# An exact LSTM solved by sweeps: the convergence test moved from the end of a sweep to its step 44

## What is computed

```python
x_proj = jnp.einsum('btd,gd->btg', x, W_ih) + b_ih + b_hh
def step(carry, xp):
    h, c = carry
    gates = xp + h @ W_hh.T
    i, f, g, o = jnp.split(gates, 4, axis=-1)
    c = jax.nn.sigmoid(f) * c + jax.nn.sigmoid(i) * jnp.tanh(g)
    h = jax.nn.sigmoid(o) * jnp.tanh(c)
    return ((h, c), h)
_, hs = jax.lax.scan(step, (h0, c0), jnp.swapaxes(x_proj, 0, 1))
```

## Time and profile before

| | |
|---|---|
| median of 3 runs | 2495.29 us (2492.91 to 2497.29) |
| the profiled execution | 2494.4 us |
| its span in the trace | 2492.6 us |
| mean granted TensorE clock | 0.953 of full speed |
| busy: PE, PE weight loads | 88%, 76% |
| busy: DVE, ACT | 69%, 60% |
| matmuls of the sweeps, line 746 | 4800 records, 602.6 us busy |

### The profile page before, as it was taken

The page is one execution under the profiler, slowest core; times in us unless marked ns, Lnnn a source line. Parts: engine busy times, 40 slices in busy tenths (PEclk is TensorE's granted clock), DMA queues, the critical chain, the costliest instruction groups (busy, mean ns, idle before and its releaser), DMA issues.

```text
span 2492.6 us, 43835 instructions
## 1 busy us (share of the span) xinstructions
PE 2193.6 (88%) x13739; PEld 1884.3 (76%) x13739; DVE 1716.5 (69%) x3984; ACT 1504.2 (60%) x3023; POOL 156.2 (6%) x156
## 2 busy tenths in 40 slices
PE   4678989999999999999989899988888888888834
PEld 2457877888888888888878688878887888788723
DVE  5755878777777777777747777765655656555685
ACT  2344448888888878888843366655554555455515
POOL 2333000000000000000000000000000000000060
PEclk7789999999999999999999999999999999999975
DMA  3212320000000000000043122223332333233203
GB/s 93 80 63 82 94 95 20 28 22 28 26 25 25 28 27 25 25 29 24 22 123 93 36 99 112 104 108 113 114 114 84 114 115 107 90 115 115 74 2 101
DMA packets 94279, 174.11 MB, mean 70 GB/s; under 512 B 8088, under 2 KB 68500, under 8 KB 93858
## 3 DMA queue, kind: packets, MB, share of 16 engines
q1 hardware_dynamic: 62914, 86.59, 10.6%
q10 hardware_dynamic: 28108, 81.19, 10.4%
q0 software_dynamic: 3136, 4.76, 0.7%
HBM read 114.14 MB, written 58.36 MB: 69 GB/s over the span
## 4 chain that ended last, share of the span: by engine, by line
PE 52%; DVE 19%; ACT 8%; issue 8%; ACTq 2%; DMA 2%; DVEq 1%; POOL 0%; POOLq 0%
PE psum L600 23%; PE psum L595 11%; PE psum L746 8%; PE psum L703 4%; DVE scr L1542 3%; DVE scr L1540 3%; ACT scr L1012 2%; ACT scr L1020 2%; DMA out_dram<-wq 2%; DVE scr L1538 2%; DVE scr L1336 2%; DVE wp L1432 2%; DVE bufB L1460 1%; DVE bufB L1544 1%; ACTq L1031 1%
## 5 line engine op out<-in xcount | busy, mean ns | idle before, releaser
L920 ACT ACTIVATE counts<-psum 125x500 fp32r<-125x500 f32 (+1 forms) x663 | 719.9, 1121 | 158.3 <-PE psum L595 156.2
L600 PE MATMUL psum<-halves,counts 125*125 125x512 f32 x2500 | 741.9, 417 | 2.5 <-ACT counts L920 2.0
L1362 DVE TENSOR_TENSOR wx<-rs_buf 128x500 bf16<-128x500 bf16 (+2 forms) x1326 | 640.8, 530 | 130.3 <-PE psum L595 76.4
L746 PE MATMUL psum<-bufB,wx 128*128 x4800 | 602.6, 283 | 80.5 <-DVE bufB L1544 71.5
L746 PEld LDWEIGHTS psum<-bufB,wx 128*128 128x128 f32 x4800 | 564.1, 193 | 118.8 <-issue 108.0
L600 PEld LDWEIGHTS psum<-halves,counts 125*125 125x125 f32 x2500 | 416.9, 186 | 59.8 <-issue 4.5
L595 PE MATMUL psum<-wx 128*125 128x250 bf16 x2550 | 398.4, 276 | 5.3 <-DVE wx L1362 5.1
L595 PEld LDWEIGHTS psum<-wx 128*125 128x125 bf16 x2550 | 319.7, 138 | 91.1 <-DVE wx L1362 8.7
L1020 ACT ACTIVATE scr<-scr 128x125 f32<-128x125 f32 x300 | 92.2, 307 | 172.3 <-DVE scr L1542 172.3
L1544 DVE TENSOR_TENSOR bufB<-scr 128x125 f32 (+1 forms) x300 | 87.1, 290 | 146.6 <-ACT scr L1020 146.6
L703 PE MATMUL psum<-bufA,wx 128*128 (+1 forms) x800 | 180.1, 376 | 3.1 <-POOL rs_buf L457 3.1
(11 more groups left out here) (249 smaller groups left out, 2230.4 us busy)
## 6 DMA issues: line engine op xcount, KB each, us to landing
bufA<-gates_of_x ACTq DMA_DIRECT2D x144, 500.0 KB, 3.4
gates_of_x<-bufB SPq DMA_DIRECT2D x24, 1000.0 KB, 3.9
sums_by_feature<-scr SPq DMA_DIRECT2D x51, 125.0 KB, 2.1
x_times_eps_plus_sums<-rs_buf ACTq DMA_DIRECT2D x10, 625.0 KB
wx<-in_x_dram SPq DMA_DIRECT2D x25, 250.0 KB
x_plus_mix<-wx SPq DMA_DIRECT2D x25, 250.0 KB, 4.9
scr<-x_times_eps_plus_sums SPq DMA_DIRECT2D x50, 125.0 KB
x_times_eps_plus_sums<-scr SPq DMA_DIRECT2D x50, 125.0 KB
```

Source lines behind the costliest of these rows:

```text
L600: return mm(psum[0:TP, 3 + v, :], cnt[v][:, hi, :], xhl[:, hi, :, :].rearrange("p s d -> p (s d)"), start=(hi == 0), stop=(hi == NT - 1))
L746: return mm(gate_half(u, m, gate), whhv[:, k, (2 * gate + m) * P:(2 * gate + m + 1) * P], h, start=False, stop=(k == 1), skip_group_check= ...
L920: fn(cnt[v][:, :, 2 * GW * u:2 * GW * u + GW * g].rearrange("p h c -> p c h"), psum[0:TP, u % 3, 0:g * KEYS].rearrange("p (c h) -> p c h", ...
L1362: last = tt(to[:, 0:gs, :, :], tab2[:, 0:k, :].unsqueeze(1).broadcast_to([P, gs, k, 2]), keysT[v][:, part_, g0:g0 + gs, :].unsqueeze(2).br ...
```

## The change

A constant CUT = 44 splits each sweep. `up_to_cut` does steps 0 to 43, `later_step` one of the steps 43 to 49 written out. Before the loop, all three engines do steps 0 to 43 of the first sweep, and DVE copies the states there into a spare buffer (`keep_cut`). One turn of the While loop now does steps 44 to 49 of a sweep, hands the end states on as new starts, does steps 0 to 43 of the next sweep, and then compares the states after step 43 (slot 44 of `hs`, and the cell state) with those that the sweep before had there. Where no element differs by more than the tolerance, the loop ends, and slots 45 to 50 keep what the sweep before wrote. The tolerance is unchanged. The core of the diff:

```diff
+CUT = 44
-        dif = rs_buf[:, 1616 + G4:1616 + G4 + 4 * (CH - 1)].rearrange("p (a j) -> p a j", a=4)
+        dif = rs_buf[:, 1616 + G4:1616 + G4 + 2 * HC].rearrange("p (a j) -> p a j", a=4)
+        at_cut = rs_buf[:, 0:2 * HC].rearrange("p (a j) -> p a j", a=4)
...
+            up_to_cut(0)
             with pe.While(lambda: pe.snap(go) > pe.snap(k_r_)):
-                with pe.Fori(0, LS // 2) as i:
-                    for u in range(2):
-                        time_step(pe.snap(base + 2 * i + u), 2 * i + u, u)
+                for t in range(CUT, LS):
+                    time_step(pe.snap(base + t), t, t % 2)
+                pe.wait_ge(S["st_v"], kv * 3 + 10)
+                up_to_cut(pe.snap(base + LS))
...
+            up_to_cut(0, 0)
             with act.While(lambda: act.snap(go) > act.snap(k_r_)):
+                for t in range(CUT, LS):
+                    later_step(base, before, t)
+                up_to_cut(act.snap(base + LS), act.snap(before + (LS // 2 - 1)))
...
+            def keep_cut():
+                dve.tensor_copy(at_cut[:, 0:2, :], hs[:, CUT, :, :])
+                dve.tensor_copy(at_cut[:, 2:4, :], cN)
+            up_to_cut(0, 0)
+            keep_cut()
...
+                for t in range(CUT, LS):
+                    later_step(base, before, t)
                 dve.wait_ge(S["hh_v"], 2 * base + (2 + 2 * LS))
+                dve.tensor_copy(init_c[:, :, 1:CH], cN[:, :, 0:CH - 1]).then_inc(S["st_v"], 1)
+                dve.tensor_copy(hs[:, 0, :, 1:CH], hs[:, LS, :, 0:CH - 1]).then_inc(S["st_v"], 1)
+                dve.wait_ge(S["st_v"], kv * 3 + 9)
+                dve.tensor_copy(cN, init_c[:, :, :]).then_inc(S["st_v"], 1)
+                dve.wait_ge(S["st_v"], kv * 3 + 10)
+                up_to_cut(dve.snap(base + LS), dve.snap(before + (LS // 2 - 1)))
+                tt(dif[:, 0:2, :], hs[:, CUT, :, :], at_cut[:, 0:2, :], ALU.subtract)
+                tt(dif[:, 2:4, :], cN, at_cut[:, 2:4, :], ALU.subtract).then_inc(S["sw_d"], 1)
...
                 ts(good[:, :], worst[:, :], TOL2, None, ALU.is_le).then_inc(S["sw_v"], 1)
+                keep_cut()
...
+            for v in range(2):
+                dve.wait_ge(S[f"pre_ld{v}"], dve.snap(k_r_) * (8 * LS - 16) + 8 * CUT)
```

More of the change, by code:

```diff
@@ L770, in time_step, with up_to_cut @@
                 half_mm(u, 1, 3, 1, h[1]).then_inc(S["ho_mm"], 1)
+            def up_to_cut(base):
+                for u in range(2):
+                    time_step(base + u if isinstance(base, int) else pe.snap(base + u), u, u)
+                with pe.Fori(1, CUT // 2) as i:
+                    for u in range(2):
+                        time_step(pe.snap(base + 2 * i + u), 2 * i + u, u)
+            up_to_cut(0)
             k_r_, go = pe.alloc_register("pe_sweeps"), pe.alloc_register("pe_go")
@@ L1035, in _, with later_step, up_to_cut @@
             loaded = [[pre_in[v][:, 0:2, :], pre_in[v][:, 2:4, :]] for v in range(2)]
[L1036 to L1043, removed]
+            def later_step(base, before, t):
+                done, u = act.snap(base + t), t % 2
+                if t < LS - 2:
+                    fetch(done, t, u)
+                if t < LS - 1:
+                    act.wait_ge(S[f"pre_ld{1 - u}"], 16 * before + 16 * ((t + 1) // 2))
+                act.wait_ge(S["hth_act"], 2 * done)
+                fill(1 - u, loaded[1 - u] if t < LS - 1 else kept[0])
+                sweep_step(done, u)
+            def up_to_cut(base, before):
                 fetch(base, 0, 0)
+                if not isinstance(base, int):
+                    act.wait_ge(S["hth_act"], 2 * base)
                 fill(1, kept[1])
                 sweep_step(base, 0)
-                with act.Fori(0, LS // 2 - 2) as i:
+                with act.Fori(0, CUT // 2 - 1) as i:
                     for u in (1, 0):
@@ L1055, in _ @@
                         sweep_step(done, u)
[L1056 to L1070, removed]
+                later_step(base, before, CUT - 1)
+            fill(0, kept[0])
+            up_to_cut(0, 0)
+            k_r_, go = act.alloc_register("act_sweeps"), act.alloc_register("act_go")
+            act.reg_mov(k_r_, 0)
+            act.reg_mov(go, CH)
+            with act.While(lambda: act.snap(go) > act.snap(k_r_)):
+                kv = act.snap(k_r_)
+                base = act.snap(kv * LS)
+                before = act.snap(kv * (LS // 2 - 1))
+                for t in range(CUT, LS):
+                    later_step(base, before, t)
+                up_to_cut(act.snap(base + LS), act.snap(before + (LS // 2 - 1)))
                 act.wait_ge(S["flag_v"], kv + 1)
@@ L1553, in _, with later_step, up_to_cut @@
             dve.memset(psum[0:1, 6, 400:401], 0.0).then_inc(S["cnt_z"], 1)
+            cN = tg_c[0][:, 1, :].rearrange("p (c j) -> p c j", c=2)
+            def later_step(base, before, t):
+                u = t % 2
+                if t < LS - 1:
+                    dve.wait_ge(S[f"pre_ld{1 - u}"], 16 * before + 16 * ((t + 1) // 2))
+                fill(1 - u, loaded[1 - u] if t < LS - 1 else kept[0])
+                sweep_step(dve.snap(base + t), t, u)
+            def up_to_cut(base, before):
+                fill(1, kept[1])
+                sweep_step(base, 0, 0)
+                with dve.Fori(0, CUT // 2 - 1) as i:
+                    for u in (1, 0):
+                        t = 2 * i + 2 - u
+                        dve.wait_ge(S[f"pre_ld{1 - u}"], 16 * (before + i) + 16)
+                        fill(1 - u, loaded[1 - u])
+                        sweep_step(dve.snap(base + t), t, u)
+                later_step(base, before, CUT - 1)
+                dve.wait_ge(S["hh_v"], 2 * base + (2 + 2 * CUT))
+            def keep_cut():
[3 more added lines that the diff above has]
+            keep_cut()
             k_r_, go = dve.alloc_register("dve_sweeps"), dve.alloc_register("dve_go")
@@ L1560, in _ @@
                 before = dve.snap(kv * (LS // 2 - 1))
[L1561 to L1570, removed]
```

12 lines of the change are left out of this document (3 added, 9 removed).

## The result

The change takes 2457.77 us, the median of four runs (2454.25 to 2461.89), against 2495.99 us of the kernel before on the same chip (four runs, 2492.91 to 2497.29). The ratio is 0.9845 with a 95% interval of 0.9833 to 0.9858: 38 us less, where 30 were forecast. The profiled execution took 2456.2 us, its span 2454.3.

What follows compares the result with a forecast made beforehand. Bound by a closed PE-ACT-DVE ring, steps times period. Terms 621.3 + 4.8 + 13.4 + 12.2 = 651.7 against 682.75 us; with a shorter passed test and one clock fall 29.9 us less: 2465.0 us, range 2460.0 to 2472.0.

Steps and rivals of the forecast that it cites:

- Three sweeps: Sweeps: the third stays the last and ends at step 43, 144 steps instead of 150; chance 89%.
- the host's 15%: Comparison after step 43 of the third sweep: host calculation gives 1.29e-5 against tolerance 1.526e-5, passing with 15% to spare.
- The closed ring: Each step: PE, ACT and DVE wait in turn, none runs ahead, so a step left out saves its whole period, 4.41 us.
- The handover's working: Step 49 to 0, twice: PE waits for the third copy and starts 2.3 us late; 13.4 us together.
- The failed test: Second sweep, step 43 to 44: the old 12.66 us interval less 0.5 us, so 12.2 us.
- The price of a fourth sweep: Rival, comparison after step 43 of the third sweep fails: one more turn, 233 us, time 2698 us; chance 10%.
- The entry into the While loop: First sweep, step 43 to 44, issued beside DVE's state copies: 0.4 us over a period, 4.8 us.
- item 1: Sweeps' normal periods fall from 147 to 139: 657.43 us becomes 621.3 us.
- One fall out of the two handovers: Handovers, PE idle some 2.6 us: PE's clock falls at one of two, +1.6 us, with 0 and +3.2 as ends.
- The price of 1.6 us: PE's start to first sigmoid after a clock fall: 3.81 us against 2.24, so each fall costs 1.6 us.
- The code fetch at the jump back: While loop's one jump back, behind the failed test: instruction fetch priced between 0 and 3.4 us, taken as 0; chance 15%.
- the Trainium skill's rule on taken branches: While loop's jump back: a taken branch outside a two-page window forces a fetch, so the longer turn would pay there.

Runs made afterwards that it cites:

- The first two experiments: Changed kernel with steps 44 to 47 back in a loop, on PE alone (2458.44 us), then on DVE alone (2463.6 us); one run each.
- the DVE run: Changed kernel with DVE's steps 44 to 47 back in a loop, h written to a slot from a register; 2463.6 us, one run.

## Why the prediction was wrong

**Right.** Three sweeps. The chip's margin after step 43 lies between 0 and 21%, by the run with the tolerance of 1.2e-5; the host's 15% is not measured more closely. The closed ring: each step left out was worth its period, since no other interval grew for it and the run with CUT = 46 was 9.7 us longer for two steps more. The handover's working, 13.4 against 13.24 us, with PE released by the third copy; two small errors in it cancel, a start 0.2 us later than put and steps around it that are shorter. The failed test, 12.2 against 11.68 us: the copies of `keep_cut` did not hold the flag back, and PE starts 1.83 us behind the flag's start (2089.82 - 2087.99) where it took 2127.93 - 2125.69 = 2.24 before. The price of a fourth sweep, 233 us: from first to last sigmoid the run with the tighter tolerance took 886.05 - 647.30 = 239 us more than the change. The entry into the While loop hid under other work nearly altogether, 4.23 us.

**Wrong: item 1, "Normal periods: 147 fall to 139".** I priced all 139 at the old mean of about 4.47 us, though ten of them (44 to 49 in two sweeps) lie between steps that the change writes out. They measured 4.14, and the other 129 the 4.47 put for them. Ten times 0.33 us is 3.3, which is the 3.1 us missing in that term but for 0.2. With them at the old price the median would have been some 2461 us, inside the range. The likely cause can be read from the order of PE's instructions, which I had looked at only for what moved. In the loop the address of h is computed between the wait (line 756 of the changed file) and the matmuls; in a written-out step nothing stands there (this is the order in the program, which no trace records):

```
loop:         L756 ISA / L748 ISA / L748 MATMUL psum<-bufB,wx 128x125 x6
written out:  L756 ISA / L748 MATMUL psum<-bufB,wx 128x125 x6
```

I took the change for a smaller number of the same steps. The first two experiments give the parts, 0.09 us on PE and 0.17 on DVE, and the old kernel with written-out steps had the same 4.14. So it is shown that the looped form of the step costs this, engine by engine. That it is the address and not something else in the looped form is argued from the order and from the later starts; no run keeps the loop and computes the address ahead of the wait.

**Half right: the clock.** "One fall out of the two handovers" is a mean and not what one run does. In the change and the eleven experiments that have handovers there are 26 of them: 13 kept the clock (5.8 to 6.6 us) and 13 lost it (7.0 to 8.3). With an idle time like the change's (2.77 to 2.87 us) it is 7 kept against 12 lost, so that the profiled execution kept both was luck. The price of 1.6 us is near the 1.5 that most falls cost, but two cost 2.7 or 2.8 (8.33 + 5.36 us in the DVE run, 8.33 + 5.44 with the tighter tolerance). What decides is open: an idle time of 2.77 us came out both ways.

**The range.** Its lower end, 2460.0, took in the runs' scatter of 2 us and a clean clock, and missed the shorter steps (3.1) and the stages ahead (2.1). Two slips stand in the last additions: 2464.5 + 0.9 is 2465.4 and not 2465.0, and 2465.0 less 1.6, 0.4 and 2 is 2461.0 and not 2460.0; with them put right the measured time lies further out. The scatter was too small: the change's four runs span 7.6 us. In all fourteen traces, which have the same code ahead, the first sigmoid lies between 1665.7 and 1674.7 us, and the tail behind the last sigmoid was 8.4 us shorter once, with CUT = 42. Such a range needs 4 to 5 us to either side for what the change does not touch.

**Not come true.** The code fetch at the jump back, which I had priced at 0 to 3.4 us and set to 0: it needed a body five times as long, and then cost 3.2 us. I had also written that by the Trainium skill's rule on taken branches ("Runtime: NRT & Kernel Launch", "Instruction fetch mechanics") the new turn would pay at its jump back; the change's trace, with no instruction packet around its failed test, does not bear that out.

## What to carry over

When a change writes loop steps out, price the new form of the step and not only their number: on this closed ring the looped form, most likely by an address computed behind the wait, cost 0.25 us in each step, and it is visible as the idle time between a releaser and its instruction. Straight code ran at full speed here, but a jump over it with nothing else to do was on the path, so write out what runs always and keep the loop that may not run short and behind it; even then, skipping that loop cost DVE some 2.6 us. Where a measured total agrees with the forecast, take it apart into its intervals first: twice here the agreement or the miss came from parts that no theory had named. A test that is known to fail is a full stop of all engines; leave it out before shortening it.

## What the runs showed of the hardware

- A step in a loop, with the slot of h from a register: PE's first matmul 0.15 us behind its releaser instead of 0.06, DVE's product 0.15 behind ACT's tanh instead of 0.03.
- A jump back over about 50 written-out steps: two instruction packets on q8 and four on q14, and 4.9 us from flag to first matmul against 1.7. With ACT's body alone so long: 3.5 us from flag to ACT's first work against 1.25, hidden at the jump back and 2.2 us on the path at the exit. Back over ten steps: none. Past a loop of the same ten steps that was never entered: DVE 4.35 us behind the flag against 1.8.
- Straight code: 25 instruction packets on q8 and 19 on q14 in 390 us, with nearly all periods at 4.14 or 4.15 us.
- Loop turns are not always on the path: every second period was longer by 0.17 us in the later sweeps (gone with ACT's loop), by 0.11 us in the first (not ACT's), and by nothing in a second sweep whose base was a constant. With CUT = 42 and 46 it was 0.10 and 0.08 in the later sweeps. What makes these differences is open.
- PE's granted clock at the handovers: behind an idle time of 2.77 to 2.87 us it stayed at 1.00 in 7 cases and fell to 0.50 in 12, at once or within 2 us of PE's start; behind 2.50 us it stayed in 2 of 3 cases, behind 1.97 to 2.34 us in all 4. Behind the failed test, with 4.0 and 1.9 us idle around one small matmul, it was at 0.50 each time.
